# Two-layer graph attention on one core: layer 1's raw features in a buffer of their own, made in half chunks during the steps, their parts made by head, and each mask turned once for each layer

## The reference

```
h = relu(layernorm(x))
# layer 0, one head: hp = h @ W0.T ; s_src, s_dst = hp @ a_src, hp @ a_dst
x = x + softmax(where(adj, leaky_relu(s_src[i] + s_dst[j], 0.2), -1e9)) @ hp
h = relu(layernorm(x))
# layer 1, four heads of 64: f = h @ W1.T + b
x = x + per head: softmax(where(adj == 1, leaky_relu(s_src[i] + s_dst[j], 0.2), -9e15)) @ f
```

## Time and profile before

| | |
|---|---|
| median of 3 runs | 3015.81 us (3013.6 to 3017.25) |
| the profiled execution | 3018.92 us, its span 3016.8 us |
| busy in the span: PE, DVE, ACT, POOL | 2547.6, 1974.3, 1658.7, 1362.7 us |
| granted TensorE clock, mean | 0.94 of full speed |
| chain that ended last, by engine | PE 61%, DVE 16%, ACT 9% |

### The profile page before, as it was taken

How to read it: one execution, slowest core, us unless ns; L and a number is a source line. 1 busy time by engine, 2 the same in 40 slices (tenths; PEclk the granted TensorE clock), 3 DMA queues, 4 the chain that set the end, 5 groups by cost and what they waited for, 6 DMA issues and landing times.

```text
span 3016.8 us, 60805 instructions
## 1 busy us (share of the span) xinstructions
PE 2547.6 (84%) x22166; PEld 2286.1 (76%) x22166; DVE 1974.3 (65%) x3342; ACT 1658.7 (55%) x3042; POOL 1362.7 (45%) x1757
## 2 busy tenths in 40 slices
PE   4987998869998699896998879987899879987586
PEld 3865888758887588875888768886788758887576
DVE  1535777468764687637776387664777657775896
ACT  3034565645656456564655565564565645555674
POOL 2112455435544355533555345543445434444566
PEclk9998999889999899998999989999999989999798
DMA  7641243042332233231332323313133132100110
GB/s 130 77 61 32 44 67 57 26 58 43 69 62 33 40 61 64 47 48 29 62 66 40 47 36 61 62 38 62 25 64 65 28 53 43 33 22 16 29 40 19
DMA packets 197798, 147.88 MB, mean 49 GB/s; under 512 B 143072, under 2 KB 144224, under 8 KB 197472
## 3 DMA queue, kind: packets, MB, share of 16 engines
q1 hardware_dynamic: 179040, 110.07, 15.5%
q0 software_dynamic: 18432, 33.56, 12.7%
HBM read 193.60 MB, written 50.66 MB: 81 GB/s over the span
## 4 chain that ended last, share of the span: by engine, by line
PE 61%; DVE 16%; ACT 9%; issue 8%; POOL 3%; DMA 2%; DVEq 1%; SPq 0%; ACTq 0%; POOLq 0%
PE accA L941 25%; PE accB L960 15%; PE accB L966 10%; DVE shared L1213 4%; PE accA L861 4%; ACT shared L756 3%; DVE shared L1167 2%; PE accB L861 2%; PE misc_ps L861 2%; DVE shared L1230 2%; PE accA L842 2%; DVE Sw L1083 2%; DMA Rb<-R_dram 1%; DVE xb L1201 1%; DVE shared L1071 1%
## 5 line engine op out<-in xcount | busy, mean ns | idle before, releaser
L756 ACT ACTIVATE shared<-Rb,dd 128x512 int8<-128x512 f32 x1616 | 1013.1, 717 | 328.2 <-DVE shared L1230 327.1
L941 PE MATMUL accA<-S,shared 128*128 128x257 f32 x4096 | 1006.5, 399 | 196.5 <-DVE shared L1167 192.8
L960 PE MATMUL accB<-Sw,shared 128*128 128x195 bf16 x7680 | 983.9, 251 | 97.1 <-DVE shared L1234 90.1
L941 PEld LDWEIGHTS accA<-S,shared 128*128 128x128 f32 x4096 | 786.1, 198 | 339.1 <-DVE shared L1167 232.8
L966 PE MATMUL accB<-Sv,shared 128*128 128x130 f16 x7680 | 768.4, 224 | 0.0
L960 PEld LDWEIGHTS accB<-Sw,shared 128*128 128x128 fp8e4 x7680 | 644.0, 99 | 141.4 <-issue 108.9
L1167 DVE SCALAR_TENSOR_TENSOR shared<-Rb,dd,mask 128x512 f32<-128x512 f32 x512 | 448.6, 891 | 301.8 <-PE accA L941 248.1
L966 PEld LDWEIGHTS accB<-Sv,shared 128*128 128x128 fp8e4 x7680 | 581.9, 99 | 1.3
L529 POOL TENSOR_SCALAR shared<-shared 128x260 f32<-128x260 f32 x128 | 123.0, 961 | 892.5 <-ACT shared L786 889.4
L1230 DVE TENSOR_TENSOR shared<-shared,mask 128x512 uint32<-128x512 uint32 x512 | 391.0, 764 | 196.1 <-ACT shared L756 176.9
L1234 DVE TENSOR_TENSOR shared<-shared,mask 128x512 uint32<-128x512 uint32 x512 | 399.6, 780 | 11.7
(11 more groups left out here) (112 smaller groups left out, 2631.5 us busy)
## 6 DMA issues: line engine op xcount, KB each, us to landing
Rb<-R_dram SPq DMA_DIRECT2D x160, 256.0 KB, 3.5
adj_bytes<-in_adj POOLq DMA_DIRECT2D x128, 256.0 KB, 6.4
xb<-in_x SPq DMA_DIRECT2D x32, 512.0 KB, 4.5
out<-xb SPq DMA_DIRECT2D x32, 512.0 KB, 3.6
mask<-adj_bytes SPq DMA_TRANSPOSE x128, 4.4
shared<-in_W SPq DMA_DIRECT2D x2, 256.0 KB, 3.0
R_dram<-R_rows SPq DMA_DIRECT2D x8, 32.0 KB, 1.8
a_cols<-in_a SPq DMA_DIRECT2D x8, 0.2 KB, 10.4
```

The costliest lines, as they stand in the source:

```text
L756: last = nc.scalar.activation(cmp[:, slot, jj // 2, of_pair(jj % 2, 0, CI)], Rb[:, h, :], ACT.Sign, bias=w[1][:, JG * g + jj, h:h + 1], sc ...
L941: last = nc.tensor.matmul(accA[:, k, 0:F + 1], tiles[:, j % RING, k * P:(k + 1) * P], S0[:, j, 0:F + 1], start=j == 0, stop=j == NJ - 1)
L960: nc.tensor.matmul(acc[:, bank, col:col + NS], bits[:, g % BRING, 1, jj // 2, of_pair(jj % 2, k * P, P)], Sw[:, j, h, :, :].rearrange("p a ...
```

## The change

`S1` and `split` get memory of their own, so layer 1's raw features of chunk c-1 are made during step c, half a chunk (two tiles) at a time: `norm_half` (event `"N1"`, ACT), `turn_half` (`"T1"`, PE, into `misc_ps`), `move_half` (`"Y1"`, ACT), `feat_half` (`"F1"`, PE, one tile), `move_half` on DVE (`"MV"`). The last chunk's halves are made in `slot_g` and at the start of `slot_f`. The parts are made by head over all 16 tiles instead of by chunk over all heads; heads 0 and 1 in `slot_f`, heads 2 and 3 within head 0 of the first step, now called `"AB1"`, where DVE compares groups 10 and 13 instead of 0 and 1, and where `"X1"` of chunk 0 moves from head 1 to head 0. To free the memory, the seven mask slots become two for each layer, and each mask is turned twice.

```
-    MSLOTS = NC + 3
+    AB_FIRST_GROUPS = [10, 13]
...
+            elif h == 0 and parts:
+                events += a[0] + a[1] + [("NM", 2), ("W", 2), ("HI", 2)] + g[0] + [("LF", 2), ("MID", 2), ("HIGH", 2)]
+                events += g[1] + [("NR", 2), ("LS", 2)] + a[2] + [("NM", 3), ("W", 3), ("HI", 3)] + load + g[2]
+                events += [("LF", 3), ("MID", 3), ("HIGH", 3), ("LOW", 2)] + a[3]
+                events += g[3] + [("NR", 3), ("LS", 3)] + early + eb + [("LOW", 3)]
...
-        S1 = part(0, NJ * E1 * 4, fp32).rearrange("p (j e) -> p j e", j=NJ)
...
-        mask = sb("mask", [P, MSLOTS, NJ // 2, 2 * CI], u8)
+        mask = sb("mask", [P, 4, NJ // 2, 2 * CI], u8)
+        S1 = sb("S1", [P, NJ, E1])
+        split = sb("split", [P, NJ, CF])
+        y1 = sb("y1", [P, 2, F])
+        yT1 = sb("yT1", [P, KC, 2 * P])
...
+            def mask_of_layer_1(n):
+                if n < CHUNKS:
+                    if n >= 2:
+                        sp.wait_ge(S["bits_ready"], HG * (n - 2) + HG)
+                    turn_mask(n, 2 + n % 2, mask1_in)
...
+            def feat_half(b, t, tile):
+                q, k = 2 * (NC * b + t) + tile // 2, tile % 2
+                pe.wait_ge(S["yt1_ready"], q + 1)
+                if k:
+                    pe.wait_ge(S["feat_moved1"], 2 * q + 1)
+                for kc in range(KC):
+                    last = nc.tensor.matmul(misc_ps[:, 0:E1], yT1[:, kc, k * P:(k + 1) * P],
+                                            WT[1][:, kc, :], start=kc == 0, stop=kc == KC - 1)
+                last.then_inc(S["feat1_done"], 1)
...
-                events = [("T", 0), ("FE", 0), ("T", 1), ("A", 0), ("FE", 1), ("T", 2), ("A", 1), ("FE", 2), ("T", 3),
...
+                events = [("A", 0), ("F1", 2), ("A", 1), ("F1", 3), ("A", 2), ("A", 3), ("MX",), ("A", 4), ("A", 5), ("MN",),
+                          ("A", 6), ("RW",)] + [("A", j) for j in range(7, NJ)]
...
-                        if h == 0:
-
-                            wait_alone(pe, S["sw_ready"], NC * (b - 1) + (g + 1))
-                            wait_alone(pe, S["sv_ready"], NC * (b - 1) + (g + 1))
                         if g == 0:
-
+                            wait_alone(pe, S["sw_ready"], H * (b - 1) + (h + 1))
+                            wait_alone(pe, S["sv_ready"], H * (b - 1) + (h + 1))
...
+            def weigh(b, h):
+                if h == 0:
+                    dve.wait_ge(S["ones_ready"], b + 1)
+                    dve.wait_ge(S["exp_ready"], 2 * layer_index(b, 1) + 2)
                 else:
-                    dve.wait_ge(S["sw_ready"], NC * b + t)
...
+                    dve.wait_ge(S["sw_ready"], H * b + h)
```

More of the change, by code:

```diff
@@ L71, in order @@
[L71 to L77 removed]
+            a = [[("A", G * h + i)] * do_a for i in range(G)]
+            g = [[("G", h, i)] * do_b for i in range(G)]
@@ L682, in parts, with part_of @@
-            def parts(b):
-                first_part(b, 0)
-                move_rows(b, 1)
-                second_part(b, 0)
-                high(b, 0)
-                for t in range(1, NC):
-                    first_part(b, t)
-                    second_part(b, t)
-                    high(b, t)
-                    low(b, t - 1)
-                low(b, NC - 1)
-            def features(b, L):
-                norm(b, L, 0, True)
-                move_yt(b, L, 0)
-                norm(b, L, 1, True)
+            def part_of(h, piece):
+                return Sw[:, :, h, piece, :]
@@ L902, in slot_f @@
[L902 to L913 removed]
+                        turn_y(b, t + 1, (t + 1) % 2)
@@ L1113, in slot_g @@
+            def slot_g(b, more):
                 events = []
```

561 lines of the change are left out of this document (292 added, 269 removed), and 11 rows, old and new, of the table events.

## The result

| | before | after |
|---|---|---|
| median of 4 runs | 3016.53 us (3013.6 to 3018.32) | 3107.56 us (3106.31 to 3109.23) |
| the profiled execution's span | 3016.8 us | 3104.5 us |
| busy in the span: PE, DVE, ACT, POOL | 2547.6, 1974.3, 1658.7, 1362.7 us | 2583.7, 1978.1, 1660.9, 1361.4 us |

The changed kernel is **slower**: ratio 1.0303, 95% interval 1.0285 to 1.0321. The forecast was 2921 us. DVE, ACT and POOL have as much to do as before; PE is busy 36 us more and idle for the rest of the 88.

What follows compares the result with a forecast made beforehand. PE was taken to bound the steps, but in `slot_f` to wait mostly for DVE's layer 0 tiles. Batches -98 + 5, start +16 + 7, end -25 gave -95: from 3018.9 to 2924, median about 2921 us, range 2835 to 2995.

Steps and rivals of the forecast that it cites:

- `slot_f`: Stage making layer 0's first chunk: two rounds of parts instead of four, 83.2 us down to 40, -43 a batch.
- first step: Step after `slot_f`: 4.4 us of features, 17 more PE waiting, 3 of lower clock; +24 a batch.
- second step: Feature work of 4.4 us, one tile of it hidden in the wait at the step's end: +3.5 a batch.
- start: Before the first `slot_f`: three `"A"` steps +16 us, first half chunk of features made in the open +7.
- the gap at the end: Between the last `slot_g` and the first `"B"` step, 63.5 us before: PE starts near 23, so -40.
- A feature tile (0.89) falls into the wait at the step's end, so 3.5 each: Steps two and three: 4.4 us of features less one hidden tile, together +7 a batch, idle at the edges unchanged.
- 3 more for matmuls that run at the lower clock: In the first step, matmuls after PE's pauses run at the lower clock, as in `slot_f`: 3 us a batch.
- rival 1: First step's wait mostly hidden, 5 us instead of 17, without the clock's 3: 84 us less, 2840 us; chance 0.25.
- Rival 2: `slot_f` stays near 52 us, held by rounds with POOL links or a late row: 3005 us; chance 0.12.
- The masks: Masks turned twice, 128 more transposing DMAs: cost 0, or 6 us a batch if their cover were gone.
- Rival 4: POOL's four instructions block DVE in the first step, 2 us each: 56 us more, 2977 us; chance 0.06.
- Rival 3: First step's parts meet ACT's comparisons and busy POOL, PE idles 34 us and more, not 18: 3033 us; chance 0.10.

Runs made afterwards that it cites:

- e1_no_hold: The changed kernel with DVE's copy of the feature tile reading no PSUM, so it never waits for PE (layer 1's features wrong): 2967.5 us.
- e5_late_moves: The changed kernel with each of DVE's four feature tile copies three groups of bits behind PE's tile, the last two in the next stage: 2952.5 us.
- e6: The changed kernel with all heads' parts in `slot_f`, DVE comparing groups 0 and 1 in the first step, and DVE's copies three groups behind: 2883.8 us.
- e4: The changed kernel with the parts of all four heads in `slot_f` and DVE comparing groups 0 and 1 in the first step: 3044.6 us.
- e2: The changed kernel with layer 1's masks turned only for the first two chunks and used again for all others (output wrong): 3107.9 us.

## Why the prediction was wrong

Per batch, term by term, forecast and measured, stages cut as the prediction cut them (`slot_f` went from 83.2 to 50.0 us, counted from the end of the last transposes ahead of its first tile; the third step from 69.9 to 78.2, `slot_g` from 75.4 to 74.7):

| term | forecast | measured | apart |
|---|---|---|---|
| `slot_f` | -43 | -33.2 | +9.8 |
| first step | +24 | +28.2 | +4.2 |
| second step | +3.5 | +11.0 | +7.5 |
| third step | +3.5 | +8.3 | +4.8 |
| `slot_g` | -2 | -0.7 | +1.3 |
| sum | -14 | +13.6 | +27.6 |

From the start of the first `slot_f` to the gap at the end, all batches together, the changed kernel takes 87 us more, where -98 + 5 = -93 was forecast: 180 of the 182 us by which the profiled execution missed its 2924. The three terms outside were near and nearly cancel: start +19.4 (forecast +23), the gap at the end from 63.5 to 32.4, so -31 (forecast -40), the last four steps +12.3 (forecast +15).

Of the 27.6 us a batch e1_no_hold gives back 18.6 (379.1 to 360.5) with DVE's wait alone, none of it in `slot_f`. `slot_f` is off by 9.8 for its own reasons.

**The step that failed** is "A feature tile (0.89) falls into the wait at the step's end, so 3.5 each", with the sentence behind it that the idle time "at the edges stays". It priced what PE does and left DVE's copy out: four instructions of 0.43 us, which look like nothing. They are in-order waits for PE. DVE's use to PE lies in being ahead of it, and three of the four copies pulled DVE back to where PE was (in the second step it waits 6.16, 5.36 and 5.28 us ahead of them). e1_no_hold and e5_late_moves show it from two sides: without the wait, or with it further back, the second step is 72.3 and 70.1 us instead of 80.3. The prediction had asked what stands behind a wait for `less_second` in the first step and never asked it of `move_half` in all the others. It had even written down as a check that PE waits nowhere for layer 1's features; that held, PE's longest wait for DVE's copy is the one of this row of its waits:

```profile
PE misc_ps L900 <- DVE S L1075: 4.7, 8, 0.6
```

And yet they cost most, because PE waits for bits, tiles and sums that stand behind them.

**The clock was put in one stage only.** "3 more for matmuls that run at the lower clock" in the first step was right in kind: there PE was busy 4.6 us less in e6 (71.34 against 75.98 us), where no pause was left, and only 1.05 of that is the feature tile that e6 has in the next step, so some 3.6 are the clock. But the second step lost 3.6 to it as well.

**The first step** was nearly right. It is 28.2 longer: idle time went from 1.1 to 19.9 us (forecast 17 more), 4.3 are the features, the other 5 are put down to the clock (forecast 3). The two longest pauses are 5.68 us ahead of the third tile and 8.54 us, the longest of the first row of waits, behind `"X1"`; forecast were 4.3 and 7.0. The place and the cause stand as predicted, and rival 1 is out. That two heads' parts would be cheaper elsewhere is what e4 and e6 add.

**`slot_f`** was mis-sized. The forecast had the first `weigh` at 12 us from the start, it stood at 19.4 (639.17, the stage begins at 619.80). PE's timeline:

```profile
623.43 1.22 PE L1002 MATMUL accA<-S,shared 128*128 128x257 f32 x2 [3.64 <-DVE shared L1210]
626.50 2.94 PE L1002 MATMUL accA<-S,shared 128*128 128x257 f32 x6 [1.85 <-issue]
...
632.00 1.05 PE L910 MATMUL misc_ps<-WT,yT 128*128 128x264 f32 x4
```

The first tile comes 3.64 us late, a pause of 1.85 follows, and the second feature tile ends 13.2 us into the stage instead of 5.4. The profile gives both only as time in which nothing is waited for ("issue": 3.23 us on DVE ahead of its first tile at 622.23, and the 1.85 here), so their cause is open; it is not DVE's wait, as e1 has the same slot. The two rounds ran as forecast: 17.7 us from the first `weigh` to the end of the second, against 17.5. From there to the next chunk's first tile it took 13.0 instead of 10.5 us, and it was not the row that ended last there (DVE waited 3.67 us for it, where the forecast had 5.6, and makes its tiles from 665.08 on) but PE's own last tiles (to 668.37) and behind them ACT, which moved the chunk's sums out of `accA`. DVE, then PE:

```profile
665.08 1.41 DVE L1210 SCALAR_TENSOR_TENSOR shared<-Rb,dd,mask 128x512 f32<-128x512 f32 x2 [3.67 <-DMA Rb<-R_dram]
```

```profile
669.80 3.73 PE L1002 MATMUL accA<-S,shared 128*128 128x257 f32 x16 [1.43 <-ACT shared L737]
```

Rival 2 (52 us) was thus nearly what happened there, with another cause than it named.

**The masks** cost nothing (e2).

**Rival 4** had its mechanism right, but not its size. In the first step of the changed kernel three of POOL's four instructions fall on DVE's. POOL, then DVE:

```profile
682.39 2.19 POOL L492 TENSOR_TENSOR S<-S,Sv 128x1040 f32<-128x1040 f32 x1 [12.61 <-ACT Sv L706]
...
697.05 2.22 POOL L492 TENSOR_TENSOR S<-S,Sv 128x1040 f32<-128x1040 f32 x1 [7.85 <-ACT Sv L706]
```

```profile
682.43 2.69 DVE L1210 SCALAR_TENSOR_TENSOR shared<-Rb,dd,mask 128x512 f32<-128x512 f32 x1
...
686.91 2.33 DVE L1278 TENSOR_TENSOR shared<-shared,mask 128x512 uint32<-128x512 uint32 x1
...
697.14 2.15 DVE L1228 TENSOR_SCALAR alone<-shared 128x4 f32 x1
```

By themselves the first two take 0.75 and 0.69 us, and the third, which belongs to `"X1"`, is among the shortest (its least is 0.15 us): DVE loses some 5.5 us in all, each time until POOL's instruction is over (the second one is POOL's `weigh` of head 3, 686.45 to 688.69). The first stands directly ahead of PE's pause of 5.68 us, the third in the block ahead of the one of 8.54, and the two pauses are 1.4 and 1.5 us longer than forecast. So this rival is the likeliest reason for what the two pauses are longer than forecast; its 8 us more a batch it did not reach. No run takes POOL's instructions away, so what they cost PE is not shown.

**Rival 3**, the only one on the slower side, had the right sign for the wrong reason: it doubled the first step's wait, which came out near the forecast.

That a copy out of PSUM can't simply go to POOL, which is behind PE anyway, is the Trainium skill's ("GPSIMD Engine Reference", section 4.1: nothing that touches PSUM goes to GpSimd); no run here shows it.
